# Squares of head groups added in pairs by GpSimd, half as many selector products on TensorE, and a shifted softmax bound

## The reference, cut to what matters

```python
x = x + xattn(layernorm(x), ctx, ctx, Wq, bq, Wk, bk, Wv, bv, Wo, bo)
x = x + ffn(layernorm(x), ...)          # 8 experts, top 2
# xattn, 16 heads of 32 numbers, 4096 queries, 3202 keys:
q, k, v = queries @ Wq + bq, keys @ Wk + bk, values @ Wv + bv
A = softmax(q k^T / sqrt(32));  out = (A v) @ Wo + bo
```

## Time and profile before

| what | value |
|---|---|
| median of 3 runs | 2495.17 us (2495.07 to 2497.3) |
| the profiled execution's own time | 2496.92 us |
| its span | 2494.8 us |
| PE busy | 2418.3 us (97%) |
| DVE busy | 2154.4 us (86%) |
| ACT busy | 1841.8 us (74%) |
| POOL busy | 400.4 us (16%) |
| mean granted TensorE clock | 0.983 of full speed |

### The profile page before, as it was taken

How to read it: one execution, slowest core, us unless ns; L and a number is a source line. 1 busy time by engine, 2 the same in 40 slices (tenths; PEclk the granted TensorE clock), 3 DMA queues, 4 the chain that set the end, 5 groups by cost and what they waited for, 6 DMA issues and landing times. The chain is left out here.

```text
span 2494.8 us, 36973 instructions
## 1 busy us (share of the span) xinstructions
PE 2418.3 (97%) x13522; PEld 1284.4 (51%) x13522; DVE 2154.4 (86%) x1941; ACT 1841.8 (74%) x2157; POOL 400.4 (16%) x512
## 2 busy tenths in 40 slices
PE   8999699999999999999999999999999999969998
PEld 7878444444444444444444444444444447758776
DVE  4368499999999999999999999999999998867555
ACT  3123399989889989898998989898899876624333
POOL 2113210100000000000000000000000003236654
PEclk9999799999999999999999999999999999979999
DMA  7436690111150011115101111500101017644463
GB/s 267 162 124 227 193 215 23 27 27 26 35 124 23 23 27 27 30 31 125 23 23 27 27 33 28 125 23 22 30 24 35 18 60 254 224 114 142 139 210 121
DMA packets 131352, 214.12 MB, mean 86 GB/s; under 512 B 26822, under 2 KB 64166, under 8 KB 130412
## 3 DMA queue, kind: packets, MB, share of 16 engines
q1 hardware_dynamic: 104268, 144.67, 20.7%
q0 software_dynamic: 24576, 59.52, 7.7%
q10 hardware_dynamic: 2336, 7.60, 0.9%
HBM read 146.36 MB, written 83.04 MB: 92 GB/s over the span
## 5 line engine op out<-in xcount | busy, mean ns | idle before, releaser
L1124 ACT ACTIVATE probs<-psum 128x1024 f32<-128x1024 f32 x1600 | 1509.0, 1035 | 148.2 <-PE psum L1275 144.2
L1275 PE MATMUL psum<-q_st,k_st 97*128 97x512 f32 x3200 | 921.7, 419 | 15.6 <-DVE k_st L943 12.3
L1275 PEld LDWEIGHTS psum<-q_st,k_st 97*128 97x128 f32 x3200 | 547.7, 188 | 592.3 <-ACT probs L1124 413.4
L1187 DVE TENSOR_TENSOR even_sums<-even_sums,probs 128x2048 f32<-128x2048 f32 x352 | 806.4, 2291 | 0.2 <-ACT probs L1124 0.2
L1296 PE MATMUL psum<-probs,v_st 128*32 128x512 f32 x6400 | 799.1, 601 | 0.0
L1187 DVE TENSOR_TENSOR odd_sums<-odd_sums,probs 128x2048 f32<-128x2048 f32 x320 | 732.1, 2288 | 1.0
L1296 PEld LDWEIGHTS psum<-probs,v_st 128*32 128x32 f32 x6400 | 152.2, 108 | 352.0 <-issue 263.9
L2056 PE MATMUL psum<-we_hi,wo 128*128 x624 | 219.3, 413 | 7.7 <-ACT wo L1895 5.2
L800 POOL DMA_DIRECT2D sum_scratch<-shared_rows x31 | 18.3, 590 | 1207.6 <-ACT shared_rows L1079 1207.6
L2056 PEld LDWEIGHTS psum<-we_hi,wo 128*128 128x128 f32 x624 | 119.8, 192 | 34.5 <-issue 8.8
L1888 ACT ACTIVATE shared_rows<-hold 128x512 f32<-128x512 f32 x78 | 63.5, 814 | 84.0 <-DMA hold<-token_rows,whole 46.0
(11 more groups left out here) (230 smaller groups left out, 2050.8 us busy)
## 6 DMA issues: line engine op xcount, KB each, us to landing
q_st<-qh_scratch SPq DMA_DIRECT2D x64, 256.0 KB
k_st<-kh_scratch SPq DMA_DIRECT2D x56, 192.0 KB, 3.7
token_rows<-rows SPq DMA_DIRECT2D x8, 1028.0 KB, 6.7
xn<-in_x SPq DMA_DIRECT2D x16, 512.0 KB, 6.5
qh_scratch<-o_hi SPq DMA_DIRECT2D x8, 1024.0 KB, 4.5
ql_scratch<-o_lo SPq DMA_DIRECT2D x8, 1024.0 KB, 7.6
q_st<-ql_scratch SPq DMA_DIRECT2D x32, 256.0 KB
token_rows<-in_x SPq DMA_DIRECT2D x1, 8192.0 KB, 37.3
```

The costliest lines, as they stand in the source:

```text
L1124: nc.scalar.activation(probs[:, p_slot(it, t), 2 * half:2 * half + 2, :], psum[:, 2 * slot:2 * slot + 2, :], ACT.Exp, scale=SCALE).then_in ...
L1187: nc.vector.tensor_tensor(into[:], a, probs[:, p_slot(it, t)], ALU.add).then_inc(added, 1)
L1275: mm = nc.tensor.matmul(psum[:, 2 * slot + h % 2, :], k_st[:, h, t * P:(t + 1) * P], q_st[b][:, h, :], start=True, stop=True)
```

## The change

GpSimd writes the square of each group into a small buffer `each` of two places, and adds the two of a pair into `squares`, now two places instead of four. That makes six instructions a chunk on GpSimd in place of four, with waits for its own earlier ones: the third square waits for the first addition (the buffer is used again), each addition for the square ahead of it. TensorE makes two products of sums a chunk in place of four. The selector has half its size and half its small memsets. The shift is (30 / SCALE - bound) in place of -bound, in the same instruction, and the limit `WIDEST` is 40 in place of 30.

```diff
-WIDEST = 30.0
+WIDEST = 40.0
+HEADROOM = 30.0
...
-        squares = sb("squares", [P, NG, CH], F32R)
-        of_head = sb("of_head", [P, NG, P], F32R)
+        each = sb("each", [P, 2, CH], F32)
+        squares = sb("squares", [P, NG // 2, CH], F32R)
+        of_head = sb("of_head", [P, NG // 2, P], F32R)
...
+        SQUARE_STEPS = NG + NG // 2
...
                         if j == 0 and summed is not None:
                             pool.wait_ge(*summed)
+                        if j == 2:
+                            pool.wait_ge(squared, c * SQUARE_STEPS + 3)
                         h = o_hi[b][:, j, 0:w].bitcast(F32)
-                        pool.tensor_tensor(squares[:, j, 0:w], h, h, ALU.mult).then_inc(squared, 1)
+                        pool.tensor_tensor(each[:, j % 2, 0:w], h, h, ALU.mult).then_inc(squared, 1)
+                        if j % 2:
+                            pool.wait_ge(squared, c * SQUARE_STEPS + (2 if j == 1 else 5))
+                            pool.tensor_tensor(squares[:, j // 2, 0:w], each[:, 0, 0:w], each[:, 1, 0:w], ALU.add).then_inc(squared, 1)
...
-                for j in range(NG):
+                for two in range(NG // 2):
                     for h in range(HG):
-                        dve.memset(of_head[h * DH:(h + 1) * DH, j, HG * j + h:HG * j + h + 1].bitcast(F32), 1.0).then_inc(selector, 1)
+                        dve.memset(of_head[h * DH:(h + 1) * DH, two, HG * two + h:HG * two + h + 1].bitcast(F32), 1.0).then_inc(selector, 1)
...
-                dve.tensor_scalar(neg_bound[:], ones_row[:, 0:1].to_broadcast([1, CH]), bound[:], -1.0, ALU.mult, ALU.mult).then_inc(neg_ready, 1)
+                dve.tensor_scalar(neg_bound[:], ones_row[:, 0:1].to_broadcast([1, CH]), HEADROOM / SCALE, bound[:], ALU.mult, ALU.subtract).then_inc(neg_ready, 1)
...
-                    pe.wait_ge(squared, (c + 1) * NG)
-                    for j in range(NG):
-                        mm = pe.matmul(psum[:, bank, 0:w], of_head[:, j, :], squares[:, j, 0:w], start=j == 0, stop=j == NG - 1)
+                    pe.wait_ge(squared, (c + 1) * SQUARE_STEPS)
+                    for two in range(NG // 2):
+                        mm = pe.matmul(psum[:, bank, 0:w], of_head[:, two, :], squares[:, two, 0:w], start=two == 0, stop=two == NG // 2 - 1)
                     mm.then_inc(summed, 1)
...
-                pe.wait_ge(selector, 2 + HEADS)
+                pe.wait_ge(selector, 2 + HEADS // 2)
```

## The result

Beside each other, 15 runs of each: 2501.5 us (2498.52 to 2504.64) against 2496.59 us (2494.35 to 2499.81) for the kernel before. The ratio is 1.002, with an interval of 1.0013 to 1.0028: 4.9 us slower. The forecast was 2498.6, 3.4 slower, with a range to 2501.2. So the direction was right, the loss was set too low, and the time lies just outside the range. Of the distance of 2.9 us, 1.4 is the base: the three runs that were shown had a median of 2495.17, the fifteen have 2496.59. The other 1.5 is an error of the sum.

The account below looks back on a forecast made before the run. TensorE, busy nearly all of the span, was taken as the bound wherever nothing else ends last. Terms +4.4 - 0.46 + 1.7 - 2.3 + 0.3 + 0 - 0.46 + 0.25 = +3.4 us on 2495.17 gave 2498.6, range 2494.6 to 2501.2.

Parts of the forecast that it names:

- First sums at 30.2: First chunk of keys: TensorE starts the sums at 30.2 in place of 25.79, +4.4 us, waiting for GpSimd's longer chain.
- GpSimd and VectorE exclude each other: First chunk of keys: VectorE's 128x2048 split shuts GpSimd out; without exclusion the delay would be +2.3 us, not +4.4.
- The clock falls, 1.7: Behind TensorE's idle time at the first chunk of keys, half clock costs 1.7 us, bounds 0 and 3.4.
- Five chunks of keys, -2.3: Second to sixth chunk of keys: additions hidden, two products fewer save 0.46 us each, 2.3 in all.
- Between keys and queries, +0.3: From keys to queries the chain goes over VectorE, slowed by two GpSimd additions: +0.3 us, between 0 and 0.8.
- Queries, 0: Six of eight query chunks: TensorE's 0.46 us turn into longer waits for VectorE's search, whose idle 1.07 covers the addition.
- rival 4: Queries: VectorE is pushed over its idle cover of 1.07 us, 0.3 lost in each of six chunks, 2500.4; chance 0.12.
- the distance from sums to sums moves: Sign against the forecast: in the queries the distance from one chunk's sums to the next was to stay unchanged.
- The end, +0.25 - 0.46: Last query chunk: addition less two half-clock products moves the search +0.25 us; no turn behind its sums gives -0.46.
- all up to the barrier moves with it: End of the projections: everything from the last search to the barrier was to move by the search's +0.25 us.
- The shift and the limit at nothing: The shift's instruction is exchanged one for one and the raised limit keeps the fallback pass out: 0 us.
- The dense score products at 302.6: Start of attention: the dense score products were to begin at 302.6 in place of 299.18 us, 3.4 later.

Follow-up runs that it names:

- second profile of the changed kernel: The changed kernel run once more, nothing altered, beside the same runs of the kernel before: ratio 1.0018 (1.0009 to 1.0027).
- quarters: The changed kernel with VectorE's 128x2048 split as four instructions of 128x512; one run, first sums 9.00 us behind the first `o_hi`.
- the one with the same input twice: The changed kernel with each GpSimd addition taking the second square twice in place of two squares; one run, 6294.48 us.

## Why the prediction was right or wrong, point by point

- **First sums at 30.2.** Right in the place, 0.5 to 0.6 short in the size: +5.0 in place of +4.4. The term that was too small is "an addition takes 1.04". It takes 1.30 and 1.26 in this chain, and the waits of GpSimd for itself took 0.08 and 0.15, not 0.05. 1.30 is the upper end of the forecast's own bound (0.9 to 1.3). The longer first addition also turned the order round: the split came ahead of the third square, not behind it. The end of the chain is the same, as GpSimd waits for the split once either way.
- **GpSimd and VectorE exclude each other.** Right. Holding the split back takes 2.1 out of the chain, quarters make the two take turns, and the split behind GpSimd's subtraction takes 6.65. The Trainium skill (SBUF — State Buffer, Who interferes with whom) calls the port pair that the two share an exclusive lock, and has a VectorE instruction with two inputs in SBUF contend with a GpSimd instruction that reads SBUF. The trace agrees (2.29 alone, 2.70, 6.65).
- **The clock falls, 1.7.** Right, and the size depends on the execution: 2.3 with 5.2 us of work at the half level in the first profile, 1.7 with 3.7 us in the second. With TensorE kept busy through the wait the clock stayed full, so the fall comes of standing idle.
- **Five chunks of keys, -2.3.** Right: -2.47 in the first profile of the changed kernel, -2.3 in the second (115.03 in place of 117.37).
- **Between keys and queries, +0.3.** VectorE's four instructions took 2.29 in place of 2.00, so the rise on VectorE was foreseen. That it cost TensorE 0.3 is not shown: with the clock full, the stretch from the seventh chunk of keys to the last of the queries took 112.27 and 112.74 without additions in it and 112.82 and 112.93 with them, of which 0.2 is lost in the queries (next point). What moved these executions against each other is something else: the time from the store to ScalarE's next start ran from 3.4 to 4.8 us over the profiles, and the clock fell there in some and not in others, in the kernel before too. It was not in the forecast as a source of spread, and should have been.
- **Queries, 0.** Right from the third sums on, where the wait for the search went from 0.2 to 0.6 and the distance stayed. Wrong ahead of them: the addition costs VectorE 1.0 and not 0.7, and the cover of 1.07 was read in the third block, where the first two have 0.78. So rival 4 happened in a small way. From the first sums of the queries to the last but one it is 82.93 to 82.98 in all five profiles without additions there, and 83.15 to 83.57 in all nine with them: +0.2 in the second profile of the changed kernel, +0.6 in the first. By the forecast's own sign (the distance from sums to sums moves) this step was wrong.
- **The end, +0.25 - 0.46.** The -0.46 came: from the first to the last `o_hi` of the last chunk it is 8.66 in place of 9.10. The search did move, by 0.9 at the full clock (4.04 against 3.15) and 0.6 at half (4.52 against 3.88), more than the +0.25, since the addition is longer and since two products fewer give only 0.46 at the full clock. But "all up to the barrier moves with it" was wrong: behind the last `o_hi` the time to attention stayed at 15.34 to 15.51. So the end is worth -0.4 and not -0.2.
- **The shift and the limit at nothing.** Right.
- **The dense score products at 302.6.** They start at 304.70 in the first profile and at 302.58 in the second (299.18 and 299.95 in the kernel before). The second number is luck in part: that execution had no fall of the clock between keys and queries, and its kernel before had one. "Nothing gives it back" can't be judged, since what follows the table load spreads by more than the change.

**What failed:** the sum. The step is the price of the addition, "I take 1.04 and keep 0.9 to 1.3": it measured 1.30 and 1.26 at the first chunk, which with GpSimd's longer waits for itself made +5.0 of +4.4, and the time at half clock came out at 1.7 to 2.3 against 1.7. So the first chunk lost 6.2 to 6.8 in place of 5.6. Its second effect is in the queries, put at 0, where the longer hold of VectorE ran over the cover of the first two blocks (+0.2 to +0.6). Against that the end gave 0.2 more than its terms, because its chain does not go over the search. Added up over the keys' gain too, the located parts are 1.4 over the forecast in the first profile and 0.5 in the second. By the medians the loss was 4.9 and 4.7 in the two comparisons, 1.5 and 1.3 over the 3.4. What is left lies in stretches that differ from execution to execution, between keys and queries and behind the barrier, and stays open. The rest of the miss of 2498.6, 1.4 us, is the base of three runs.

The row that should have decided the price was there: the large subtraction has two different inputs as the addition has, the square does not. I had a quarter of it, 1.1, and still took the square's. But a quarter would have been too little as well: 4.54 for 2048 and 1.30 for 512 don't go by length alone. The Trainium skill's figure (GPSIMD Engine Reference, Performance versus the Vector engine) fits the 4.54 of 2048 elements, and the estimate of 1.12 from it falls short of 1.30 in the same way.

## What to carry to other kernels

A cheaper sum on the busiest engine pays only in the chunks where that engine sets the pace; write down for each kind of chunk (first, steady, next phase, last) what stands between the new producer's end and its consumer, and read the cover in each of them, not in one. Work moved to an engine with 16% load can still be the longest chain at the first chunk, where nothing covers it, and a stall of some us can cost half as much again in the clock. Follow a chain to what it holds up: at the last chunk the search came 0.6 to 0.9 later and attention did not. Here the steady part of the keys gave 2.3 and the first chunk took 6.2 to 6.8; with the first chunk left as it was, a loss of 0.2% became a gain of about 0.1% (0.9986 to 0.9993 in three measurements, one of which can't be told from no change).

## What the runs showed of the hardware that was not expected

- On GpSimd the same addition of 128x512 takes 1.26 to 1.31 in the first chunk with two different inputs and 1.04 with one input twice, which is also what a square takes.
- A 128x2048 subtraction on VectorE took 2.29 us with nothing of GpSimd's under way, 2.70 behind a square begun 0.5 us ahead of it, and 6.65 behind a 128x2048 subtraction begun 0.08 ahead of it.
- Behind a wait of TensorE of 4.66 us the clock came back after 5.2 us of work in one execution, and behind one of 5.76 after 3.7 in another.
- The load of the shift was issued 8.3 to 8.4 us behind the last load of the first queries in 13 profiles (8.5 in the one with the same input twice), whether its own store was issued 3.9 or 5.4 us ahead of it.
- The same kernel's executions spread over some 5 us (2494.35 to 2499.81), and their profiles differ in whether the clock falls between keys and queries: at 1.00 throughout in one, 6.8 us at half in another. What decides it stays open.
